# A four-layer network with routed experts: weight splitting in the second layer's routing stage, and the order of a norm in the third layer's attention

## The reference

```python
# layer 1, feed-forward: one expert for each token, 8 experts, hidden width 1024
aff = x @ centroids.T
eid = argmax(aff, axis=-1)
alpha = sigmoid(sum(x * centroids[eid], axis=-1, keepdims=True))
xln = layernorm(x) * ln_g[eid] + ln_b[eid]
ffn = sum over e of onehot[:, e] * (relu(xln @ w1[e] + b1[e]) @ w2[e] + b2[e])
out = x + alpha * ffn

# layer 2, attention: the tokens are the latents, 4 heads of 64
xn, ln = layernorm(context) * g + b, layernorm(latents) * g + b
q, kv = ln @ W_q, concatenate([xn @ W_kv, ln @ W_kv])      # keys: 77 of the context, 256 latents
qn, kn = rmsnorm(q, q_gamma) * SCALE, rmsnorm(k, k_gamma)  # for each head
attn = softmax(where(mask, qn @ kn.T, -max))
out = (attn @ v) @ W_out + b_out
```

## Time and profile before

| | |
|---|---|
| three runs | 1390.15, 1390.92, 1392.39 us; median 1390.92 |
| profiled execution | 1390.4 us, span 1388.7 us |
| busy share of the span | PE 75%, VectorE 58%, GpSimd 43%, ScalarE 40% |
| granted TensorE clock, mean | 0.859 of full |
| transfers | 123.47 MB, mean 89 GB/s |
| routing stage of layer 1 | from about 604 to 659 us of the span |
| latent attention of layer 2 | from about 857 to 1066 us of the span |

### The profile page before, as it was taken

How to read it: one execution, slowest core, us unless ns; L and a number is a source line. 1 busy time by engine, 2 the same in 40 slices (tenths; PEclk the granted TensorE clock), 3 DMA queues, 4 the chain that set the end, 5 groups by cost and what they waited for, 6 DMA issues and landing times. The chain is left out here.

```text
span 1388.7 us, 26577 instructions
## 1 busy us (share of the span) xinstructions
PE 1041.1 (75%) x8492; PEld 774.3 (56%) x8493; DVE 803.3 (58%) x1763; ACT 561.4 (40%) x1319; POOL 597.8 (43%) x746
## 2 busy tenths in 40 slices
PE   5777378884558888740799916798887689997998
PEld 3666167883336666630699912455555367776443
DVE  4666154442655877865455545455554538775876
ACT  2462023431126566533334305556552247774000
POOL 1473605565235667657000062556652247763000
PEclk9986589996669999955899966889898789997999
DMA  3463218862041111147777521000000100000000
GB/s 106 119 183 113 87 43 309 289 234 86 29 163 30 36 34 35 35 130 239 254 252 257 193 69 54 1 1 1 0 1 8 39 8 20 16 17 5 16 23 23
DMA packets 70682, 123.47 MB, mean 89 GB/s; under 512 B 15481, under 2 KB 41859, under 8 KB 70595
## 3 DMA queue, kind: packets, MB, share of 16 engines
q1 hardware_dynamic: 63011, 101.64, 22.5%
q0 software_dynamic: 7584, 20.72, 4.4%
HBM read 52.98 MB, written 24.64 MB: 56 GB/s over the span
## 5 line engine op out<-in xcount | busy, mean ns | idle before, releaser
L303 ACT ACTIVATE xnT<-bank 128x256 f32<-128x256 f32 (+1 forms) x112 | 42.2, 381 | 90.7 <-PE bank L292 89.4
L2411 PE MATMUL bank<-l0f_x_high,l_weights 128*128 128x256 bf16 x256 | 51.7, 320 | 34.0 <-issue 20.8
L2820 POOL DMA_DIRECT2D l_results<-keep x23 | 12.5, 544 | 135.3 <-DVE keep L2923 135.3
L3182 PE MATMUL bank<-l_weights,room 128*128 x552 | 65.1, 273 | 4.3 <-DVE room L3210 2.8
L3170 PE MATMUL bank<-room,xnT 128*128 128x128 bf16 x1104 | 67.1, 222 | 0.0
L3170 PEld LDWEIGHTS bank<-room,xnT 128*128 128x128 bf16 x1104 | 65.3, 99 | 0.3
L882 PE MATMUL bank<-ident,l_weights 128*77 128x128 f32 x256 | 39.7, 298 | 33.0 <-DVE l_weights L1073 28.3
L2243 DVE SCALAR_TENSOR_TENSOR l3f_total<-bank,l3f_share,l3f_total 128x256 f32<-128x256 f32 x112 | 54.2, 484 | 15.6 <-PE bank L2161 11.6
L2626 PE MATMUL bank<-room,l0r_placed 128*128 128x128 bf16 x936 | 61.5, 224 | 0.0
L1783 POOL TENSOR_TENSOR l2x_probs<-l2x_probs,l2x_inverse 128x333 f32<-128x333 f32 x64 | 49.5, 796 | 25.4 <-DVE l2x_inverse L1688 25.4
L3182 PEld LDWEIGHTS bank<-l_weights,room 128*128 128x128 bf16 x552 | 52.7, 98 | 12.3 <-issue 5.4
(11 more groups left out here) (430 smaller groups left out, 3252.0 us busy)
## 6 DMA issues: line engine op xcount, KB each, us to landing
xnT<-l_weights SPq DMA_DIRECT2D x23, 1024.0 KB, 5.0
l0r_placed<-l_weights SPq DMA_DIRECT2D x39, 512.0 KB, 3.6
room<-in_L_ffn_weights SPq DMA_DIRECT2D x20, 512.0 KB, 5.0
l0w_staging<-in_L_ffn_weights SPq DMA_DIRECT2D x16, 480.0 KB, 3.8
l_weights<-in_L_ffn_weights SPq DMA_DIRECT2D x16, 384.0 KB, 3.1
room<-l_rows SPq DMA_DIRECT2D x39, 128.0 KB, 3.1
l_results<-room POOLq DMA_DIRECT2D x39, 128.0 KB, 3.1
l_rows<-l_weights SPq DMA_DIRECT2D x16, 184.0 KB, 2.2
```

The source lines that it names most:

```text
L303: act.activation(self.chip.xnT[:, :, span(t, P)], bank[:, 0:DIM].rearrange("p (k n) -> p k n", k=KD), ACT.Copy).then_inc(self.copied, 1)
L2411: last = pe.matmul(self.bank[:, c, branch * width:(branch + 1) * width], self.weights[w][:, at:at + P], x[:, s, k, :], start=(i == 1), sto ...
L3182: last = pe.matmul(bank[:, 2 + u, 0:DIM], h[:, u, c * P:(c + 1) * P], expert_part(split[:, w, :, :], e, KD * hidden_width + c * DIM, DIM), ...
```

## The change

Routing stage: the staging slots become eight, four in `chip.room` and four in `chip.xnT`, which nothing reads once the logits are there. Loads, high parts and low parts go piece by piece. All 20 low parts are VectorE's, behind its chain; GpSimd only scatters. SyncE issues pieces 0 to 3, waits for the logits, issues pieces 4 to 7 ahead of the columns, then the rest.

Latent attention: ScalarE squares tile 1 of b + 2 right behind its projection copies; VectorE does `rms_sums` of tile 1 right behind `rms_norm` of tile 0, and `rms_norm` of tile 1 behind the copy of pair 2, ahead of the inverse and maxima of pair 3.

```diff
@@ latent_attention, scalar: batch @@
                 for u in range(TPB):
                     if ahead >= 2:
                         copy_projections(b + 2, u)
+                        if u == 1:
+                            square_projections(b + 2, u)
                     if u == 1 and not (first or second):
                         norm.scalar(act, TPB * b - 2 * TPB + 1, 1)
                     if ahead >= 1:
                         exponents(b + 1, 1 + u)
-                    if ahead >= 2:
+                    if ahead >= 2 and u == 0:
                         square_projections(b + 2, u)
                     copy_probsT(b, 1 + u)
@@ latent_attention, vector: batch @@
                 if ahead >= 2:
                     rms_norm(b + 2, 0)
+                    rms_sums(b + 2, 1)
                 if behind:
                     update_x(TPB * b - TPB, 0)
                 copy_probsT(b, 2)
+
                 if ahead >= 2:
-                    rms_sums(b + 2, 1)
-
+                    rms_norm(b + 2, 1)
                 if ahead >= 1:
                     invert_sums(b + 1, 2)
                     maxima(b + 1, 3)
                 if behind:
                     update_x(TPB * b - TPB + 1, 1)
                 copy_probsT(b, 3)
-                if ahead >= 2:
-                    rms_norm(b + 2, 1)
@@ relu_experts @@
-        chunk, slots = 1024, 4
-        group = slots
+        chunk, slots, in_room = 1024, 8, 4
         first = split_before // chunk
-        groups = (EXPERTS * per_expert // chunk - first) // group
-        by_gpsimd = groups // 2
-
-        staging = chip.room[:, 0:slots * chunk].rearrange("p (s n) -> p s n", s=slots)
+        pieces = EXPERTS * per_expert // chunk - first
+
+        spare = chip.xnT[:, :, :].rearrange("p k n -> p (k n)")
+        staging = [span_of[:, n * chunk:(n + 1) * chunk] for span_of, many in ((chip.room, in_room), (spare, slots - in_room))
+                   for n in range(many)]
...
+        def load_weights(sp, c):
+            wait(sp, w_split[c % slots], c // slots)
+            sp.dma_start(staging[c % slots], a["L1_ffn_weights"][:, span(first + c, chunk)]).then_inc(w_loaded[c % slots], 16)
+
+        def high_part(act, c):
+            act.wait_ge(w_loaded[c % slots], 16 * (c // slots) + 16)
+            act.activation(high[:, span(first + c, chunk)], staging[c % slots], ACT.Copy).then_inc(high_ready, 1)
+
+        def low_part(dve, c):
+            dve.wait_ge(high_ready, c + 1)
+            dve.tensor_tensor(low[:, span(first + c, chunk)], staging[c % slots], high[:, span(first + c, chunk)],
+                              ALU.subtract).then_inc(w_split[c % slots], 1)
@@ sync @@
-                load_weights(sp, 0)
+                for c in range(in_room):
+                    load_weights(sp, c)
+                sp.wait_ge(logits_ready, 1)
+                for c in range(in_room, slots):
+                    load_weights(sp, c)
                 sp.dma_start(columns[:, :, :], a["L1_ffn_columns"]).then_inc(columns_loaded, 16)
...
-                for g in range(1, groups):
-                    load_weights(sp, g)
+                for c in range(slots, pieces):
+                    load_weights(sp, c)
@@ scalar @@
-                for g in range(groups):
-                    high_parts(act, g)
+                for c in range(pieces):
+                    high_part(act, c)
@@ vector @@
                 sort.vector(dve, chain, [mask], bank[:, 1, :], bank[:, 2, :])
-                for g in range(by_gpsimd, groups):
-                    low_parts(dve, g)
+                for c in range(pieces):
+                    low_part(dve, c)
@@ gpsimd @@
-                for g in range(by_gpsimd):
-                    low_parts(pool, g)
                 pool.wait_ge(sort.slots_ready, 1)
```

## The result

The changed kernel takes 1365.53 us (median of four runs, 1362.03 to 1370.64) beside 1390.54 for the kernel before (four runs, 1385.03 to 1392.39). The medians are 25.0 us apart. The ratio, estimated with its 95% interval, is 0.9847 (0.9811 to 0.9883): 21 us less, between 16 and 26. A second measurement of the same two kernels, with more runs, gave 0.9871 (0.9827 to 0.9914), 18 us. Forecast were 19 us, from 1391 to 1372.

What follows compares the result with a forecast made beforehand. No engine bounds throughout: routing waits for GpSimd's scatters behind its own low parts, attention for VectorE's late second norm. 1390.4 - 12 - 7 = 1371.4, with 0.5 to the median 1371.9, said as 1372; range 1364 to 1381.

Steps and rivals of the forecast that it cites:

- The tail behind the last one: Routing stage: 3.54 us from the last scatter to the next stage's first transfer.
- The weights' branch: Routing stage: 12.6 MB at 354 GB/s, last low part done at 646, next stage's first transfer at 647.5.
- the two branches: Routing stage: weights and scatters each lead to 647.5 for the next stage's first transfer; 647 taken, 12 us gained.
- Rival 4: Latent attention: TensorE stays at full clock without idle stretches, some 5 us more gained, 1367; chance 0.15.
- Starved scatters (1): Routing stage: scatters find no gaps between VectorE's low parts; 1386.5, or 1378.5 for half of it; chance 0.15.
- No faster loads (2): Routing stage: loads stay at 239 GB/s, gain 4 + 7, 1380; chance 0.08.
- A wait that only changes its name (3): Latent attention: delayed maxima and copy cost all that the earlier norm gave; 1379; chance 0.12.
- (5): Routing stage: lock held through all low parts, scatters follow, 10.7 us lost there; 1394.6 in all; chance 0.02.
- (6): Routing stage and latent attention: nothing happens in either, the first wait is replaced in full; 1390; chance 0.03.

Runs made afterwards that it cites:

- e4: Changed kernel with four staging slots in place of eight, and without the wait for the logits; ratio 0.9894.
- e9: Changed kernel with both engines' last copies of probabilities earlier and pieces of 512 columns in 16 slots; 1359.92 us, ratio 0.9775.
- e10: Changed kernel, but VectorE starts its low parts only when all scatters have landed; one execution took 1383.26 us.
- e7: Changed kernel with eight slots, but the first eight low parts on GpSimd ahead of its scatters, as before; ratio 0.9942.
- e5: Changed kernel with the last pair's probabilities copied one step earlier on both ScalarE and VectorE; ratio 0.9767.
- e12: Changed kernel with only ScalarE's copy of the last pair's probabilities moved ahead of its exponents; ratio 0.9837.
- e1: Kernel before with only the routing stage's edit, latent attention unedited; 1322.77 us, ratio 0.987.
- e2: Kernel before with only the latent attention edit, routing stage unedited; 1328.96 us, ratio 0.9936.
- e3: The kernel before once more, unedited; ratio 0.9993.
- e8: Changed kernel, but VectorE multiplies by the second tile's norm last in the batch, as before; squares and sums stay early; ratio 0.989.
- e6: Changed kernel with pieces half as wide, 512 columns in 16 slots; ratio 0.9822.

## Why the prediction was right

The forecast was 19 us, from two places. In the first pair of profiles these two places gave 12.0 and 6.1 us, 18 together, and the second measurement of the whole kernels says 18. The mechanisms were the forecast ones; that the sum came so close is in part luck, as terms were off inside it and made up for each other. The other 7 us between the first two profiles belong to stages without an edit, and the forecast has no share in them.

**Routing: 12 us forecast, 11.97 measured in the first pair, 10.7 to 12.4 over all.** The steps, from the copy of the counts: slots ready at 2.7 us, as forecast (615.0 less 612.27); first scatter at 3.1 for 2.7; the first low part at 4.4 for 4.2. The scatters were taken at 1.8 us each, the middle of 1.26 and 2.4; they went by 1.83 on the mean (27.5 by 15), made up of 2.27 while VectorE ran without a pause and 1.3 to 1.8 later. The middle was a choice between two bounds, not a derived value: that it fits is luck, and for a scatter that just misses one end, where I had 2.4, the measured step is 2.27. The tail behind the last one is 3.2 for 3.54.

Two terms were off and made up for each other. The weights' branch was to be through at 33.7 us behind the counts (646); it was through at 29.5. I priced all bytes at 354 GB/s and put refill, high and low part behind them; the window shows 371, and some of the scattered rows move only after the last piece. And between the last low part and the next load I allowed 1.5 us; e4 shows 0.27. So the two branches were not equal, as I had it: the scatters ended last by 2 us, with 3.2 behind them. Had they gone by 1.26, the weights would have set about 30 us; e9 comes near, where the last low part ends at 30.8 and the load comes 0.6 behind it. "What is late next is the weights' transfer, then the scatters" was the wrong way round.

The sentence of the Trainium skill that was weighed (SBUF — State Buffer, Who interferes with whom: descriptor generation should not starve under a tensor_tensor, for a reason that the page itself marks as inferred) is contradicted again: e10 against the changed kernel, 0.96 us on the median for 1.41. Its exclusive lock fits e7, where VectorE's operation took 2.17 us beside GpSimd's and 0.29 without.

**Attention: 7 us forecast.** A batch was to gain 1.2 us, from 20.5 to 19.3; it gained 1.26, in every steady batch of each kernel with exactly this edit (e5 and e9, with both copies moved, gained 2.5). The waits of 13.8 us became 6.9 for the copy and 3.0 for what is left of the norm, in two waits of the start-up. The wait that I named as the new one was VectorE's copy; the trace puts the time down to ScalarE's, and e12 shows that both stand there. Over the stage the changed kernel gained 6.1 us. From the first to the last group of L1336 it is 9.8 (146.2 to 136.4 us), helped by two slow batches (23.5 and 22.1) in the first profile, for one (22.2) in the second; 0.9 is lost ahead of the first group, and 2.8 are given back at the end, where the granted clock is 0.84 in the last 23 us of the stage and was 0.99 in the same stretch before:

```profile
1036.76 1.92 PE L1387 MATMUL bank<-room,l2x_mixedT 128*128 128x256 f32 x4
```

The same four took 1.03 elsewhere. The slow batches go with the clock too: 0.84 of full in the one from 982 to 1002 us before, 0.85 in the one from 901 to 923.2 us after, 0.99 and 1.00 in the neighbours. Without a slow batch on either side, e1 against e2 on one chip, the groups of L1336 span 138.8 and 130.2 us: 8.7 less with the edit, a little over the forecast 7 (the stage's mean clock is 0.92 in both).

The late stretch at the lower clock may or may not belong to the edit. From the last L1336 to the end of the stage it is 39.3 to 39.4 us in the kernel before, e3, e5, e8 and e9 and 40.6 in e12, but 42.1 to 43.9 in the changed kernel and its repeat, e2, e4, e6, e7, e10 and also e1, which has no edit to attention. So the edit is not needed for it, but every profile with exactly this order of attention has it, and three of the four without the edited norm order (before, e3, e8) do not. What decides it I did not settle; the wait of 1.80 us ahead of these products is the same before and after the change. Single profiles show 210 to 215 us for one program order. Rival 4, 5 us more from the clock, did not come in them; by windows over the whole stage, before and then changed:

```profile
845.90:1066.90 221.00, 183.04 (x980) 111.19 (x980) 115.49 (x328) 114.92 (x368) 115.58 (x154) 0.91 0.00 1
```

```profile
830.60:1045.60 215.00, 183.24 (x980) 112.76 (x980) 114.10 (x328) 113.72 (x368) 113.06 (x154) 0.90 0.00 1
```

TensorE is busy as long as before, 183 us, and the granted clock is no higher: the 6 us are idle time that is gone.

**The rivals.** Starved scatters (1): in the changed kernel's profile not one was held beyond the end of the low part that ran when it was issued; the gather of the earlier trace rows, which found no gap in several operations, remains the exception. No faster loads (2): refuted by 371 GB/s. A wait that only changes its name (3): nearly half true, 1.05 of 2.42 us, as the forecast itself had it. (5) and (6) did not come.

## What to carry to other kernels

When two engines share work beside a chain that releases a third thing, look whose list stands ahead of the release: GpSimd's low parts cost 17 us of queue ahead of the scatters, and from the counts to the slots VectorE's chain took 10.7 us beside them for 2.7 without. Where an engine's short, urgent operation must slip in between another's long ones, the spacing of the long ones sets its pace in whole steps; halving them took 2.5 to 3 us off the stage here. And where two copies or waits end together, move both at once, or a test of one will say that it does not matter.

## What the runs showed of the hardware that was not expected

A scatter beside back-to-back low parts goes in whole multiples of their spacing: 2.27 us is two of 1.14, 1.80 is three of 0.60. Where a scatter and a low part are recorded as starting within 0.02 us of each other, either can go first; seven scatters in a row that did (e9) were not slowed at all and went by 1.26.

The same program took 1338 us on one chip and 1390 on another, and all of the difference is in layer 0: 351.6 us for 403.4, every other stage within 3.1 us (before and e3). In the slower chip's profile of the kernel before, by its timeline, ScalarE, VectorE and TensorE stand in the shared experts' part around 140 to 200 us for nothing that the profile names (`remote`: the semaphore event that ended the wait belongs to no instruction in the profile):

```profile
150.19 0.38 ACT L2444 ACTIVATE l0f_s_squash<-bank 128x256 f32<-128x256 f32 x1 [10.94 <-remote]
...
170.81 0.38 ACT L2444 ACTIVATE l0f_s_squash<-bank 128x256 f32<-128x256 f32 x1 [18.36 <-remote]
```

It is the same in the kernel before and in the changed one on that chip, so it is no part of the change. Its cause was not looked for.
